# Gate logits from one 32-column stationary tile: four matmuls per batch for six, and a sum on VectorE

## The reference

```
logits = jnp.einsum('bsd,ed->bse', hidden_states, gate_w)      # 16 experts
scores = jax.nn.softmax(logits, axis=-1).transpose(0, 2, 1)
topk_w, topk_idx = jax.lax.top_k(scores, cap)                  # cap = 64 of 512 tokens
...                                                            # gather, gelu(x Wg) * (x Wu), Wd, times topk_w, scatter-add
shared = (gelu(h Ws_g) * (h Ws_u)) Ws_d                        # for every token
out = x + gb * (experts + shared)
```

## Time and profile before

| | before |
|---|---|
| runs: median (lowest to highest) | 2468.5 us (2468.02 to 2469.97) |
| profiled execution: span | 2465.3 us |
| profiled execution: own time | not listed apart from the runs; the span lies 3.2 us under their median |
| instructions in the trace | 40995 |
| TensorE matmul, busy | 2372.3 us, 96% |
| VectorE, busy | 1567.9 us, 64% (902.6 of the 1190 us from 100 to 1290, 76%) |
| ScalarE, busy | 1032.8 us, 42% |
| GpSimd, busy | 1150.4 us, 47% |
| one iteration of phase A without a round | 38.07 us (234.13 to 272.19, starts of `x_transposes`) |
| one iteration with a round | 38.20 us (615.74 to 653.94) |

### The profile page before, as it was taken

How to read it: one execution, slowest core, us unless ns; L and a number is a source line. 1 busy time by engine, 2 the same in 40 slices (tenths; PEclk the granted TensorE clock), 3 DMA queues, 4 the chain that set the end, 5 groups by cost and what they waited for, 6 DMA issues and landing times.

```text
span 2465.3 us, 40995 instructions
## 1 busy us (share of the span) xinstructions
PE 2372.3 (96%) x14388; PEld 2086.3 (85%) x14388; DVE 1567.9 (64%) x3198; ACT 1032.8 (42%) x1912; POOL 1150.4 (47%) x997
## 2 busy tenths in 40 slices
PE   6999999999998999999987999999999999999997
PEld 5888888888887888888876888888888888888886
DVE  6677767778776877788846455555554545555553
ACT  3545545444553545545442333333333333333332
POOL 1233333333332333333352666666666666666664
PEclk9999999999998999999998999999999999999999
DMA  2111111111111111111115444443444444434433
GB/s 90 53 44 59 51 60 60 52 51 57 54 61 44 60 43 60 52 60 60 59 62 90 86 90 82 88 84 66 79 84 87 86 85 88 84 60 86 84 62 43
DMA packets 78506, 167.03 MB, mean 68 GB/s; under 512 B 11744, under 2 KB 46720, under 8 KB 78368
## 3 DMA queue, kind: packets, MB, share of 16 engines
q0 software_dynamic: 49152, 67.14, 16.7%
q1 hardware_dynamic: 29216, 97.85, 11.8%
HBM read 97.71 MB, written 67.24 MB: 67 GB/s over the span
## 4 chain that ended last, share of the span: by engine, by line
PE 84%; DVE 6%; issue 4%; POOL 2%; DMA 1%; ACT 1%; SPq 0%; DVEq 0%; POOLq 0%; ACTq 0%
PE ps L349 26%; PE ps L351 26%; PE ps L350 26%; PE ps L501 2%; DVE stage L856 2%; PE ps L387 1%; DVE bn_stats L758 1%; PE ps L420 1%; DMA stage<-in_wd 1%; DVE x_t L753 1%; PE ps L442 1%; DVE hidden L753 1%; POOL rstd L1144 1%; POOL out L1209 1%; ACT x_t L693 0%
## 5 line engine op out<-in xcount | busy, mean ns | idle before, releaser
L349 PE MATMUL ps<-x_t,weights 128*128 128x512 f32 x1536 | 617.3, 402 | 23.2 <-DVE hidden_f L1111 13.3
L350 PE MATMUL ps<-x_t,weights 128*128 128x512 f32 x1536 | 602.5, 392 | 0.0
L351 PE MATMUL ps<-x_t,weights 128*128 128x512 f32 x1536 | 601.8, 392 | 0.0
L1209 POOL DMA_INDIRECT out<-x_rows,step_token x256 | 418.1, 1633 | 333.9 <-DVE x_rows L1090 275.4
L349 PE MATMUL ps<-weights,hidden 128*128 128x256 f32 x1536 | 435.8, 284 | 8.7 <-POOL hidden L1148 5.6
L351 PE MATMUL ps<-weights,hidden 128*128 128x256 f32 x1536 | 436.1, 284 | 0.0
L350 PE MATMUL ps<-weights,hidden 128*128 128x256 f32 x1536 | 436.0, 284 | 0.0
L1111 DVE TENSOR_TENSOR hidden_f<-gelu,ps 128x512 f32<-128x512 f32 x256 | 175.7, 686 | 379.0 <-ACT gelu L733 348.1
L733 ACT ACTIVATE gelu<-ps 128x512 f32<-128x512 f32 x256 | 152.8, 597 | 535.8 <-PE ps L351 508.4
L349 PEld LDWEIGHTS ps<-x_t,weights 128*128 128x128 f32 x1536 | 290.6, 189 | 83.6 <-DVE hidden_f L1111 13.5
L1148 POOL TENSOR_TENSOR hidden<-hidden_f,hidden 128x512 fp32r<-128x512 f32 x128 | 165.5, 1293 | 408.7 <-ACT hidden L647 408.7
(11 more groups left out here) (174 smaller groups left out, 4436.9 us busy)
## 6 DMA issues: line engine op xcount, KB each, us to landing
x_rows<-in_x SPq DMA_DIRECT2D x32, 512.0 KB, 3.5
pairs<-mod_rows SPq DMA_DIRECT2D x32, 512.0 KB, 4.3
h_rows<-stage SPq DMA_DIRECT2D x32, 512.0 KB, 2.6
out<-y_rows SPq DMA_DIRECT2D x32, 512.0 KB, 2.9
stage<-in_wg SPq DMA_DIRECT2D x16, 512.0 KB, 3.4
stage<-in_wd SPq DMA_DIRECT2D x16, 512.0 KB, 4.4
stage<-in_wu SPq DMA_DIRECT2D x16, 512.0 KB
x_rows<-h_rows,step_token POOLq DMA_INDIRECT x256
```

Source lines behind the costliest of these rows:

```text
L349: pe.matmul(o, lhs(HI), rhs(HI), start=start, stop=False)
L350: pe.matmul(o, lhs(HI), rhs(LO), start=False, stop=False)
L351: return pe.matmul(o, lhs(LO), rhs(HI), start=False, stop=stop)
L1209: pool.indirect_dma_start(out=out_rows, out_offset=bass.IndirectOffsetOnAxis(ap=ICUR[g][:, t:t + 1], axis=0), in_=X1[:, g % 2, t * D:(t + ...
```

## The change

The two parts of the gate weight lie side by side, so that 16 HI and 16 LO columns are one stationary tile of 32. `gate` multiplies it with the HI and the LO rows, for each of the two k tiles: four matmuls for six. The result has 32 rows: rows 0 to 15 are the products with the weight's HI part, rows 16 to 31 those with its LO part (LO x LO, which `mm3` leaves out, is now included). ScalarE copies 32 rows for 16, and the four transposes give 32 columns each. VectorE adds the two halves with a new `tensor_reduce` from PSUM into the SBUF tile `gate_logit_sums`, raises `glog_ready` and waits for it; the maximum and the subtraction then read that SBUF tile, where they read PSUM before. The lines behind the edit move down by two to five.

```diff
--- before.py
+++ after.py
@@ -69,7 +69,7 @@
         V = sb("v", [P, 2, T, D], F32R)
         ROTK = sb("rot_k", [P, 2, KD, P], F32R)
         ROTV = sb("rot_v", [P, 2, KD, P], F32R)
-        GW = sb("gate_w", [P, 2, KD, E], F32R)
+        GW = sb("gate_w", [P, KD, 2, E], F32R)
         H1_T, H2_T = XT
         HID = H[0]
         A_T = H[1]
@@ -124,8 +124,9 @@
         NSQ = sb("norm_squares", [P, T])
         FAC = sb("out_factor", [P, T])
         GMX = sb("gate_max", [P, T])
-        GLT = sb("gate_logits_t", [E, S])
+        GLT = sb("gate_logits_t", [2 * E, S])
         GL = sb("gate_logits", [P, T, E])
+        GLS = sb("gate_logit_sums", [P, T, E])
         GEX = sb("gate_exp", [P, T, E])
         GS = sb("gate_sum", [P, T])
         GR = sb("gate_rsum", [P, T])
@@ -171,6 +172,7 @@
         h2t_done, h2t_hi, h2t_lo = map(sem, ("h2t_done", "h2t_hi", "h2t_lo"))
         gate_done, gate_read, gate_t_done, gmax_ready, gl_ready, gexp_done, gsum, grs, sg_ready = map(
             sem, ("gate_done", "gate_read", "gate_t_done", "gmax_ready", "gl_ready", "gexp_done", "gsum", "grs", "sg_ready"))
+        glog_ready = sem("glog_ready")
         gu_done, gelu_done, mul_done, hid_hi, hid_lo = map(
             sem, ("gu_done", "gelu_done", "mul_done", "hid_hi", "hid_lo"))
         down_done, y_read, y_ready, y_stored = map(sem, ("down_done", "y_read", "y_ready", "y_stored"))
@@ -449,15 +451,16 @@
                 for k in range(KD):
                     wait(pe, h2t_hi, n * KD + k + 1)
                     wait(pe, h2t_lo, n * KD + k + 1)
-                    mm = mm3(PD[0:E, 512:512 + S], lambda a: GW[:, a, k, :], lambda a: H2_T[:, a, k, :],
-                             k == 0, k == KD - 1)
+                    for part in (HI, LO):
+                        mm = pe.matmul(PD[0:2 * E, 512:512 + S], flat(GW[:, k, :, :]), H2_T[:, part, k, :],
+                                       start=k == 0 and part == HI, stop=k == KD - 1 and part == LO)
                 mm.then_inc(gate_done, 1)
 
             def gate_transposes(n):
                 wait_apart(pe, gate_read, n + 1)
                 for t in range(T):
-                    mm = pe.transpose(PD[:, 512 + t * E:512 + (t + 1) * E], GLT[:, t * P:(t + 1) * P],
-                                      IDENT[0:E, 0:E])
+                    mm = pe.transpose(PD[:, 512 + t * 2 * E:512 + (t + 1) * 2 * E], GLT[:, t * P:(t + 1) * P],
+                                      IDENT[0:2 * E, 0:2 * E])
                 mm.then_inc(gate_t_done, 1)
 
             def gate_up(n, fc):
@@ -698,7 +701,7 @@
                 if valid(i - 1):
                     act.wait_ge(gate_done, i)
                     wait(act, gate_t_done, i - 1)
-                    act.copy(GLT[:, :], PD[0:E, 512:512 + S]).then_inc(gate_read, 1)
+                    act.copy(GLT[:, :], PD[0:2 * E, 512:512 + S]).then_inc(gate_read, 1)
                     hidden(i - 1, 0)
                 if valid(i):
                     squares(i, (0, 1))
@@ -820,8 +823,8 @@
 
             def gate_weights():
                 dve.wait_ge(gate_in, 16)
-                link(dve.tensor_copy(GW[:, HI, :, :], GWF[:, :, :]))
-                split_lo(GW[:, LO, :, :], GWF[:, :, :], GW[:, HI, :, :]).then_inc(gw_ready, 1)
+                link(dve.tensor_copy(GW[:, :, HI, :], GWF[:, :, :]))
+                split_lo(GW[:, :, LO, :], GWF[:, :, :], GW[:, :, HI, :]).then_inc(gw_ready, 1)
 
             def modulations():
 
@@ -924,10 +927,12 @@
 
             def gate_max(n):
                 dve.wait_ge(gate_t_done, n + 1)
-                logits = PD[:, 512:512 + T * E].rearrange("p (t e) -> p t e", t=T)
-                dve.tensor_reduce(GMX[:, :], logits, AX.X, ALU.max).then_inc(gmax_ready, 1)
+                halves = PD[:, 512:512 + T * 2 * E].rearrange("p (t a e) -> p t e a", t=T, a=2)
+                dve.tensor_reduce(GLS[:, :, :], halves, AX.X, ALU.add).then_inc(glog_ready, 1)
+                dve.wait_ge(glog_ready, n + 1)
+                dve.tensor_reduce(GMX[:, :], GLS[:, :, :], AX.X, ALU.max).then_inc(gmax_ready, 1)
                 dve.wait_ge(gmax_ready, n + 1)
-                dve.tensor_tensor(GL[:, :, :], logits, GMX[:, :].unsqueeze(2).to_broadcast((P, T, E)),
+                dve.tensor_tensor(GL[:, :, :], GLS[:, :, :], GMX[:, :].unsqueeze(2).to_broadcast((P, T, E)),
                                   ALU.subtract).then_inc(gl_ready, 1)
 
             def gate_scores(n):
```

## The result

The change is slower, by less than a third of what was forecast: 2475.99 us median (2469.12 to 2482.61, 20 runs) against 2470.03 us (2465.21 to 2473.77, 20 runs) of the kernel before on the same chip, ratio 1.0023 with a 95% interval of 1.0015 to 1.0032. Forecast were 2487.5 us and a range from 2482. The profiled execution took 2471.89 us, with a span of 2470.1 us; before, the span was 2465.3 us.

What follows compares the result with a forecast made beforehand. TensorE, 96% busy, was taken to wait before `x_transposes` for VectorE's L856, and in rounds before `gate_up 2`. Loss 20 x 1.02 = 20.4 us, gain 1.4, net +19.0 on 2468.5: 2487.5 us, range 2482 to 2492.5.

Steps and rivals of the forecast that it cites:

- Part 1: TensorE's gate, four matmuls for six: no gain in 29 iterations that wait before `x_transposes`, 1.4 us in the other three.
- Part 2: New sum on VectorE: 284 ns, delaying what follows by 0.30 us, reaching TensorE in full in 20 iterations with a round.
- Part 3: VectorE's subtraction, now with two SBUF inputs, held until GpSimd's `hidden_lo` ends: 1.02 us delay including the sum, 20 iterations.
- Held not at all: Rival, 8%: the subtraction on VectorE escapes the hold, so the sum alone counts: +4.6 us, 2473.1 us.
- Held, but hidden: Rival, 3%: `gate_up 2` doesn't wait for `hidden 1`, so the delay costs nothing; only 1.4 us gain remains, 2467.1 us.
- TensorE's time counts in full: Rival, 4%: before `x_transposes`, L856 follows TensorE and VectorE's lateness finds slack; 14.7 us gained, 2453.8 us.
- An unpriced extra: Rival, 2%: the program's new length changes TensorE's 5.2 us issue stretch either way; 2 us allowed in the range.

Runs made afterwards that it cites:

- the change with the early addition: The changed kernel with GpSimd's addition (L1183) moved ahead of `rstd`: 2428.77 us, ratio 0.984 to the kernel before.
- halves added by TensorE, early addition: Kernel before with four gate matmuls, halves added by TensorE through two stacked identities, and GpSimd's addition L1183 moved ahead of `rstd`: 2446.45 us, ratio 0.9907.

## Why the prediction was wrong

- **Part 1, right.** Four matmuls for six gained nothing in 29 iterations: the wait grew from 13.0 to 25.2 us, 29 times 0.42, and an iteration without a round still takes 38.07 us. With the wait away the same edit is worth 0.42 us an iteration. No run measures the 1.4 us of the other three iterations by themselves.
- **Part 2, right.** 284 ns for the sum. With the sum alone (in PSUM) the iteration with a round takes 38.55 - 38.20 = 0.35 us more; I had 0.30.
- **Part 3, right in cause and size.** Held until 0.08 us behind `hidden_lo`, 897 ns in the mean, 1.02 us in each of 20 rounds; with one operand in PSUM it isn't held. "Held not at all" and "Held, but hidden" are out.
- **"TensorE's time counts in full", out**, by the same doubled wait; it comes true once the addition of L1183 is out of the way.
- **The step that failed: "An unpriced extra".** I named the program's new length and the one issue stretch of 5.2 us, gave it 2 us either way and 2%, and took the 5.2 us as all that the profile had of it. That stretch hardly moved (4.99 us). What moved were a second one of 1.8 us behind it, the time that TensorE then ran at half its clock (17.07 to 6.83 us), and a hitch at each jump back of the second half's loop: 6.2 us in iteration 18 and 7.7 in the loop, 13.9 together, against the 2 allowed. With the instructions at their old places the measured ratio is 1.0069 (1.0057 to 1.0082), where the sum of the three parts is 1.0077.

The kernel before showed it: 110 packets of instructions on its page, 56 of them between 1500 and 2400 us, and six issue waits there. I read TensorE's waits only up to 1300 us, since the change lies in that half. And that view has the second stretch as a row of its own, which I passed over:

```profile
PE ps L351 <- issue: 1.8, 1, 1.8
```

Of the clock I had noted that it is full in nearly all of phase A; the exception is the 17 us behind this stretch. An edit that makes code shorter moves all code behind it, however far off.

## What to carry to other kernels

An operation moved from PSUM to SBUF can cost more than the operation removed: count each VectorE instruction's SBUF inputs against what GpSimd runs at that time. Work taken from the busiest engine is worth nothing ahead of a wait that another chain ends; take the wait away first, and price the edit again. Where a program has long loops (1787 instructions here), compare differences of under half a per cent only after looking at the packets of the instruction queue and at the granted clock behind long waits, or with padding that keeps the old places, counted in the built program.

## What the hardware showed that I had not expected

- The place of TensorE's code in the program, and the clock behind a wait that goes with it, are worth up to 14 us of 2470. A loop of 1787 instructions was loaded again, nine packets of 16 KB, at all six jumps back (begin at 8957, 8973, 9021, 9085), at some (8901, 8925), or at two at most in most kernels that have it at 8893 or 9149 (packets in the window 2, 11, 11, 12, 19; the change with the early addition had 37). The count may differ between two profiles of one kernel, 2 and 11.
- The stretch of iteration 18, where one loop of the first half ends and another begins, took between 6.6 us (halves added by TensorE, early addition) and 13.8 us (before) more than an iteration. In all 17 profiles that is the sum of its issue waits, half of the time that TensorE worked at the low clock (0.5 of full speed granted), and 0.3 to 0.8 us. The second wait (1.5 to 1.9 us) goes with the place: the four kernels with the code of the first half where the kernel before has it show it, the 13 others don't. The low clock lasted 17.07 or 13.65 us in those four and 3.41 to 13.65 in the others (13.65 in both kernels with the sums in PSUM and in the first with the halves added by TensorE, 10.24 behind the wait of 9.50 us). What sets its length stays open; the changed kernel had 6.83 us in one profile and 3.41 in the other.
- Waits on a semaphore long set cost TensorE 0.10 us per instruction where many stand in a row ahead of its work: 64 of them 6.7 us, 192 of them 19.8 us. Four ahead of each gate cost nothing that the trace shows.
